# A fourth buffer for B and C, three results written in place, and each load one group further ahead

## The reference

```python
x = _layernorm(x + attn(x))            # a state-space block
x = _layernorm(x + xattn(x, ctx, ctx)) # retention: masked q.k products times v, no softmax
x = _layernorm(x + ffn(x))             # 16 experts, the top 2, and a shared expert

# attn: the recurrence over 64 positions, 256 inner channels, 16 states
A_bar = exp(delta[..., None] * -exp(A_log))
Bx = delta[..., None] * B_in[:, :, None, :] * xc[..., None]
h = a_t * h + bx_t
y_t = einsum('bds,bs->bd', h, c_t) + D_param * xc_t
y = y * silu(z);  return y @ W_out

# xattn
q, k, v = x @ Wq, ctx @ Wk, ctx @ Wv;  q = xpos(q);  k = xpos(k)
out = ((q @ k^T) * decay_mask) @ v
```

## Time and profile before

| | |
|---|---|
| median of 3 runs | 1173.52 us |
| the profiled execution | 1174.27 us, of which span 1172.2 us |
| mean granted clock of TensorE | 0.967 of full |
| VectorE busy | 1065.3 us, 91% of the span |
| TensorE busy | 1055.3 us, 90% |
| ScalarE busy | 993.9 us, 85% |
| GpSimd busy | 972.0 us, 83% |
| DMA queue of SyncE | 193.33 MB, 48.8% of the time of 16 DMA engines |

### The profile page before, as it was taken

How to read it: one execution, slowest core, us unless ns; L and a number is a source line. 1 busy time by engine, 2 the same in 40 slices (tenths; PEclk the granted TensorE clock), 3 DMA queues, 4 the chain that set the end, 5 groups by cost and what they waited for, 6 DMA issues and landing times. The chain is left out here.

```text
span 1172.2 us, 18321 instructions
## 1 busy us (share of the span) xinstructions
PE 1055.3 (90%) x5831; PEld 742.9 (63%) x5831; DVE 1065.3 (91%) x1492; ACT 993.9 (85%) x2176; POOL 972.0 (83%) x590
## 2 busy tenths in 40 slices
PE   4677888989899998989989899998989999898998
PEld 2465665666666666666666666666666667666665
DVE  2999999999999999999999999999999999999622
ACT  6788898989989898998979898898989889898443
POOL 0687888979988897988979798898989889897944
PEclk9677999999999999999989999999999999999999
DMA  6443444545564444555534455654545655443322
GB/s 173 175 171 146 163 164 158 164 164 189 198 196 156 172 162 153 188 207 190 182 127 168 163 189 187 204 175 162 159 160 178 208 187 182 144 166 144 122 68 74
DMA packets 84112, 194.50 MB, mean 166 GB/s; under 512 B 17288, under 2 KB 47936, under 8 KB 67632
## 3 DMA queue, kind: packets, MB, share of 16 engines
q1 hardware_dynamic: 84016, 193.33, 48.8%
HBM read 179.14 MB, written 5.77 MB: 158 GB/s over the span
## 5 line engine op out<-in xcount | busy, mean ns | idle before, releaser
L936 POOL TENSOR_TENSOR read<-state,bc_all 128x1024 f32<-128x1024 f32 x256 | 604.0, 2364 | 140.8 <-DVE state L805 126.3
L805 DVE TENSOR_TENSOR_SCAN state<-decay,drive_bank 128x512 f32<-128x512 f32 (+1 forms) x464 | 594.7, 1313 | 0.4
L755 ACT ACTIVATE decay<-delta,a_neg 128x252 f32<-128x252 f32 x1024 | 424.6, 494 | 0.9
L797 DVE TENSOR_TENSOR drive_bank<-dx_bank,bc_all 128x512 f32<-128x512 f32 (+1 forms) x496 | 328.9, 701 | 27.6 <-DMA bc_all<-bc_dram 25.8
L372 PE MATMUL y_bank<-ident,read 128*128 128x128 f32 x2048 | 282.6, 283 | 44.9 <-POOL read L936 44.8
L372 PEld LDWEIGHTS y_bank<-ident,read 128*128 128x128 f32 x2048 | 241.7, 146 | 118.9 <-POOL read L936 80.8
L977 POOL TENSOR_TENSOR hid<-gu,comb_all 128x512 f32<-128x512 f32 (+1 forms) x136 | 165.0, 1214 | 22.5 <-DVE gu L897 18.8
L363 PEld LDWEIGHTS down_bank<-down_w,hid 128*128 128x128 f32 x1024 | 132.3, 196 | 37.0 <-issue 28.1
L363 PE MATMUL bank<-x2T,gate_w 128*128 128x512 f32 (+1 forms) x272 | 135.0, 588 | 9.8 <-ACT delta L735 4.3
L363 PE MATMUL down_bank<-down_w,hid 128*128 128x128 f32 x1024 | 139.1, 281 | 3.0 <-POOL hid L977 1.4
L363 PE MATMUL bank<-x2T,up_w 128*128 128x512 f32 (+1 forms) x272 | 130.0, 571 | 0.8 <-ACT xc L711 0.7
(11 more groups left out here) (128 smaller groups left out, 1385.0 us busy)
## 6 DMA issues: line engine op xcount, KB each, us to landing
bc_all<-bc_dram SPq DMA_DIRECT2D x128, 1024.0 KB, 5.3
comb_all<-comb_dram SPq DMA_DIRECT2D x240, 128.0 KB, 3.0
x_in<-in_x_dram SPq DMA_DIRECT2D x15, 256.0 KB, 5.7
ctx_in<-in_ctx_dram SPq DMA_DIRECT2D x15, 256.0 KB, 6.4
k_pair<-k_pair SPq DMA_DIRECT2D x30, 128.0 KB, 2.1
q_pair<-q_pair SPq DMA_DIRECT2D x30, 128.0 KB, 2.5
out_dram<-y_out SPq DMA_DIRECT2D x15, 256.0 KB, 3.1
comb_all<-comb_dram SPq DMA_DIRECT2D x32, 64.0 KB, 2.6
```

The source lines that it names most:

```text
L755: done = e.activation(seqs(decay_t[j % DECAYS][:, i, h, :])[:, :, 1:T], seqs(delta[c % 2][:, h, sub * SUB:(sub + 1) * SUB])[:, :, 1:T], AC ...
L797: e.tensor_tensor(drive_bank[:, a:b, :, :], dx_bank[:, :, :].unsqueeze(1).to_broadcast(shape), bc_all[group % BC_BUFS][:, 0, PAIR * i + a: ...
L805: e.tensor_tensor_scan(states(state_t[j % STATE_BUFS], a, b), states(decay_t[j % DECAYS], a, b), states(drive_bank, a, b), 0.0, ALU.mult, ...
L936: e.tensor_tensor(read_t[j % READS][:, :, :, :], state_t[j % STATE_BUFS][:, :, :, :], bc_all[group % BC_BUFS][:, 1, PAIR * i:PAIR * (i + 1 ...
```

## The change

`BC_BUFS` goes from 3 to 4, and the load at tick 8t is of group t + 3 in place of t + 2. Three tiles are given up: `y_gated` (the product goes back to `gate_z`), `k_t` and `q_t` (the sums go back to `k_pair[:, 0]` and `q_pair[:, 0]`). The waits follow the tiles: ScalarE's copies to `k_pair` and `q_pair` wait for the scores of the chunk before, and its silu to `gate_z` for TensorE's transposes of the chunk before; VectorE's product and GpSimd's sums wait for nothing of the chunk before.

```diff
-DECAYS, STATE_BUFS, READS, BC_BUFS, COMBS = 7, 2, 2, 3, 3
+DECAYS, STATE_BUFS, READS, BC_BUFS, COMBS = 7, 2, 2, 4, 3
+BC_AHEAD = 3
...
-        y_gated = sb("y_gated", [P, SUBS, SUB_BLOCKS, INNER])
...
-        q_t, k_t = sb("q_t", [P, CHUNK]), sb("k_t", [P, CHUNK])
...
-                                        y_gated[:, sub, q, h * P:(h + 1) * P])
+                                        gate_z[:, sub, q, h * P:(h + 1) * P])
...
-                        done = mm(bank.t[:, cols], k_t[:, cols], q_t[:, cols])
+                        done = mm(bank.t[:, cols], k_pair[:, 0, cols], q_pair[:, 0, cols])
...
                 for c in due(tick, "k_copy"):
                     w.wait_ge(S["k_mm"], at(c))
-                    w.wait_ge(S["k"], at(c - 1))
+                    w.wait_ge(S["score_mm"], at(c - 1))
...
                 for c in due(tick, "q_copy"):
                     w.wait_ge(S["q_mm"], at(c))
-                    w.wait_ge(S["q"], at(c - 1))
+                    w.wait_ge(S["score_mm"], at(c - 1))
...
                 for c, sub in due(tick, "gate_z"):
                     w.wait_ge(S["z_mm"], subs_before(c) + sub + 1)
-                    w.wait_ge(S["y_gated"], subs_before(c))
+                    w.wait_ge(S["yT_mm"], subs_before(c))
...
-                    w.wait_ge(S["yT_mm"], subs_before(c))
-                    e.tensor_tensor(y_gated[:, sub, :, :], gate_z[:, sub, :, :], y_bank[:, :, :],
+                    e.tensor_tensor(gate_z[:, sub, :, :], gate_z[:, sub, :, :], y_bank[:, :, :],
...
-                    w.wait_ge(S["score_mm"], at(c - 1))
-                    e.tensor_tensor(k_t[:, 0:width(c)], k_pair[:, 0, 0:width(c)], k_pair[:, 1, 0:width(c)], ALU.add).then_inc(S["k"], 1)
+                    e.tensor_tensor(k_pair[:, 0, 0:width(c)], k_pair[:, 0, 0:width(c)], k_pair[:, 1, 0:width(c)], ALU.add).then_inc(S["k"], 1)
...
-                if tick % (GROUP_STEPS * TICKS) == 0 and 0 <= (group := tick // (GROUP_STEPS * TICKS) + 2) < ALL_SUBS * GROUPS:
+                if tick % (GROUP_STEPS * TICKS) == 0 and 0 <= (group := tick // (GROUP_STEPS * TICKS) + BC_AHEAD) < ALL_SUBS * GROUPS:
```

More of the change, by code:

```diff
@@ L963, in _ @@
                     w.wait_ge(S["q_rot"], at(c))
-                    w.wait_ge(S["score_mm"], at(c - 1))
-                    e.tensor_tensor(q_t[:, 0:width(c)], q_pair[:, 0, 0:width(c)], q_pair[:, 1, 0:width(c)], ALU.add).then_inc(S["q"], 1)
+                    e.tensor_tensor(q_pair[:, 0, 0:width(c)], q_pair[:, 0, 0:width(c)], q_pair[:, 1, 0:width(c)], ALU.add).then_inc(S["q"], 1)
                 for c in due(tick, "ret"):
```

## The result

The changed kernel took 1146.37 us in the median of its first four runs (1144.24 to 1162.05), against 1173.33 us for the kernel before; the ratio is 0.976, with a 95% interval of 0.973 to 0.979. That ratio is of the fast runs alone and leaves out the first, slow one of 1162.05 us; the two medians as they stand give 0.977. The changed kernel was measured twice more: 0.9796 (0.9766 to 0.9826) and 0.9780 (0.9751 to 0.9810). So 27.0 us were won in the first measurement, and 20.9 were forecast. The median of these four runs, 1146.37 us, lies under the low end of the forecast's range (1148.0). Over the fifteen runs of all three measurements that are left when the longest is set aside, the median is 1148.5 us, some 25 us less than before; eight of the fifteen lie above 1148.0.

The account below looks back on a forecast made before the run. VectorE was taken as the bound, held up mostly by late loads. -23.3 + 2.4 = -20.9 us took the profiled 1174.27 to 1153.4, less 0.75 for the median: 1152.6 us, own range 1148 to 1157, 8 in 10 to 1160.

Parts of the forecast that it names:

- the charge of 2.4 us: VectorE's product `y_gated` waiting for TensorE at a half-chunk's start: 0.6 us added in each of four chunks.
- The bound and the loads: VectorE sets the pace; its 23 steady-part waits for loads of B and C, 23.3 us, should all go.
- The results in place: VectorE's product and GpSimd's sums written in place: taken as 0, bounds 1.8 us and 0.1 us.
- The stand behind the store: SyncE waits at the load reading a store's rows: about 1 us, at most some 2.5, in fifteen chunks; nothing lost.
- Rival one: TensorE takes over: half of 23.3 us becomes waits for `y_bank` or the experts' banks; 1161.8 us, chance 0.13.
- Rival two: No gain: each VectorE wait replaced by another, GpSimd's queue or the banks; 1173.5 us, chance 0.05.
- Rival three: Slower: SyncE stands so long at the load behind the store that later loads are late; near 1216 us, chance 0.04.

Follow-up runs that it names:

- loads moved: Kernel before, three buffers and nothing in place, with two of three `comb_all` pairs per chunk moved behind the B and C load they held up: 1175.26 us, ratio 1.0017.
- the version with three buffers: Changed kernel with three buffers of B and C instead of four, loads still three groups ahead: 1347.36 us, ratio 1.147 to the kernel before.

## Why the prediction was wrong, and where it was right

The mechanism came true: the late loads were what was lost, and the change took them all away. The time of the first measurement fell below the range. The step that failed is the charge of 2.4 us for waits of `y_bank`, and two terms that the sum put at nothing came out at 1.6 and 1.0 us; these make 3.5 us, and the rest is scatter of the runs.

*The bound and the loads: right.* VectorE was the bound, 23.3 us of its time were waits for late loads, and all 23 went. Of the change itself, both the buffer and the place are needed: the buffer alone is worth nothing (1.0004), the place alone costs 174 us, the results in place are worth nothing (1.0008). That the loads were late by the `comb_all` waits in the one queue is shown twice from the other side, by six and by four of those buffers.

*The charge of 2.4 us: wrong, and the step that failed.* The forecast charged 0.6 us of `y_bank` wait in each of four chunks, since VectorE would come earlier to a TensorE at its limit. The term was mis-sized, and its sign was wrong for that wait: it fell from 4.3 us to 0.6 and 0.4. What the charge overlooked stands in the waits of TensorE from 129.9 to 1080 us. The kernel before:

```profile
PE y_bank L372 <- POOL read L936: 27.9, 23, 1.9
```

and the changed one (third measurement):

```profile
PE y_bank L371 <- POOL read L934: 12.4, 11, 1.8
```

Every late load held VectorE, then GpSimd's `read`, then TensorE: 15.5 us less of that, so TensorE too comes earlier to the end of a sub-chunk. That this is why `y_bank` is in time there is an argument; what the profiles show is that the two mostly go together. With late loads the `y_bank` waits are 4.3, 5.8, 1.7 and 4.6 us (before, in place only, buffer only, loads moved), in the six undisturbed profiles without them 0.2 to 0.7, and in the first run's 1.5. The 1.7 with late loads and the 1.5 without nearly meet, so the rule has its exceptions, and the cause stays open.

*A slower TensorE does cost, elsewhere.* Take a chunk from the start of TensorE's sums for its second sub-chunk to that of the next, between 190 and 1040 us. In the six undisturbed profiles without late loads, 57 chunks have no stretch at 1.2 GHz: most take 65.7 us, some up to 67.6, and the mean is 65.9. The six with one stretch of 3.4 us take 67.1 to 67.7, in the mean 67.2, the nine with two of them 68.7 to 70.8. In the kernel before and the three versions that keep the late loads, 30 chunks without such a stretch take 67.8 us in the mean and 13 with one 68.3. So one stretch costs some 1.3 us without late loads and some 0.5 with them: there a TensorE that was slow hid in part behind a load that was late. The forecast's reasoning held (what VectorE loses to a slow TensorE shows once the loads are on time), but it named the wrong wait, and left out that the old one would go. The cost varies with the run: the waits for silu are 1.0 us in the third measurement and 5.7 in the second. It is also most of the difference between these two: their spans differ by 5.6 us, and VectorE's idle time between its first product and last scan is 9.7 and 14.9 us, before 34.1.

*The sum as it came out.* From first product to last scan it was 1071.9 us before and 1045.6 and 1051.3 after, 23.5 less in the mean of the two. Of that, 21.8 are idle time: 23.3 of late loads and 4 of `y_bank` gone, 5.5 of other waits come. All waits but those for loads together so came to 1.5 us more, where 2.4 were charged; the charge missed its own wait by some 6 us, and the sum by 0.9. Another 1.6 are busy time, 1037.8 us before and 1035.9 and 1036.4 after, which the forecast left as it was; an instruction that follows without a wait starts 0.09 us before the one ahead ends (847.53 + 1.27 against 848.71), and one that has waited does not. That would give at most 23 x 0.09 = 2.1 us; but the version with 13 waits for loads has 1037.7 too, with nearly as many waits in all as the kernel before (32 and 34), so the 1.6 us are not settled. The part after the last scan is 1.0 us shorter (70.7 to 69.8 and 69.5), also put at nothing. The three terms, 0.9 + 1.6 + 1.0 = 3.5 us, lead from the 20.9 of the forecast to the 24.2 by which these two spans are shorter in the mean, with the 0.2 us of the later start. What the first four runs won beyond that, up to 27.0 us, did not come again in the two later measurements: it is scatter.

*The range.* It ended at 1148.0, two us beyond the full 23.3. The three runs of the kernel before that were known spread over 3.8 us; 29 later ones spread over 12.6 (1166.67 to 1179.31), and the changed one's fifteen over 8.8. The low end had no room for this, and over all fifteen runs the median lies only 0.5 us above it.

*The rest.* The results in place: 671 and 674 ns, right. The stand behind the store: 2.1 us in two chunks, less than forecast, with nobody behind it. Rival one: no wait for TensorE took over; the one for `y_bank` is 0.6 and 0.4 us where it wanted 12, and none for the experts' banks stands in VectorE's steady part, only the 1.0 and 5.7 us by way of silu. Rival two, no gain, is out: the ratio is below 0.983 in all three measurements. Rival three: what it describes, a load that stands so long that those behind it are late, is real in this queue, as the version with three buffers shows (+174 us), but with four buffers the wait is as short as it was.

## What to carry to other kernels

Where one queue issues all loads in a fixed order, look not at the late load but at what waits in the queue ahead of it: in this kernel the semaphore wait of one transfer was the lateness of the next. The cheapest cure may be a buffer for the small transfer that waits (here one number for `comb_all`) rather than for the large one that is late. An earlier place in the queue and a further buffer were worth something only together, and an earlier place alone made the load the one that all others waited for. When waits on the bounding engine are taken away, do not add a charge for its other waits without asking whether their releasers were held up by the same thing.

## What the runs showed of the hardware

Where VectorE is the bound and no load is late, one stretch of 3.4 us at 1.2 GHz made a chunk of 65.7 us 67.1 to 67.7 us long, and two of them in one chunk, 24 us apart, 68.7 to 70.8. One of the pairs is that at 964 and 988 us of the second measurement, shown above.

The first run of the changed kernel (1162.05 us) holds a chunk of 75 us that no later profile shows. A stretch of it, columns as in the earlier trace rows:

```profile
670.00:680.00 10.00, 6.62 (x37) 4.69 (x36) 7.34 (x9) 5.84 (x12) 7.55 (x5) 0.86 1.00 286
```

And TensorE's wait for x, in 660 to 700 us:

```profile
PE bank L371 <- DMA x_in<-in_x_dram: 3.4, 1, 3.4
```

The 16 DMA engines are busy all of these 10 us at 286 GB/s, and TensorE waits 3.4 us for the 256 KB of `x_in`, the next chunk's x. The Trainium skill (DMA: Bandwidth & Descriptors, Issuing engines are not separate DMA queues) says that transfers from all issuing engines run on the same 16 DMA engines and interleave. Here SyncE issues them all. That fits a crowd of transfers as the cause, but which of them was slow, and why in this run only, stays open.
